# Attention with a top-2 mixture of experts on one core: two tiles' scores moved in TensorE's steady order, and one tile's masking moved on VectorE

## The chip, the cores and the metric

One core of one Trainium2 chip. The metric is the device time of one execution in microseconds. The engines are named as in the profile: PE (TensorE matmuls), PEld (TensorE weight loads), DVE (VectorE), ACT (ScalarE), POOL (GpSimd), SP (SyncE, which here only issues DMAs).

## What is computed

The input x is 8 batches x 512 rows x 128 columns, fp32. With B = 8, T = 512:

```python
xn = layernorm(x)
q, k, v = xn @ Wq.T, xn @ Wk.T, xn @ Wv.T
attn = (q @ k.T) * tril(ones)            # masked scores become 0, not -inf
attn = softmax(attn / sqrt(T)) @ v
gates = softmax(xn @ Wg)                 # 8 experts, the two largest kept, renormalized
ffn = sum_e gate[e] * (xn @ We[e] + be[e])
out = x + attn + ffn
```

A masked score is zero and still takes part in the softmax, so each row also gets exp(-max) times the sum of the values behind the diagonal. The kernel adds that, and the expert biases, with one small matmul per batch (the bias product).

## The kernel before, in words

All inputs lie in SBUF from the start (one DMA per batch of x). A batch has four tiles of 128 rows. The five engines each run a list written out by hand, and they meet only at semaphores. A batch n goes through these steps; each is a function in the engine's section.

- TensorE: `transpose_x` (L302), `project_u` (u = x Wq.T Wk, L310 to L313), `wide(n, k, t)` with k = C (values, last expert, gates; 264 columns), A (four experts, 512 columns) and B (three experts, 384 columns), `scores(n, t)` (128(t+1) columns), `transpose_probs` (L277), `attend` (L293; fp32, two matmul instructions for each of its t+1 products), `value_sums` (L320), `transpose_rows` (L328) and `bias` (L334). `wide` and `scores` go through the helper `three` (L239, L240, L243): operands split into a high and a low part, three matmuls. The wide blocks, X, U, SV and DT share a ring of four PSUM banks, the scores have three banks, and attention products and the bias product gather in one bank, `attb`.
- VectorE: `mask_scores` (L560: masks the scores in PSUM and takes their maximum; a second instruction reads the accumulator), `negate_max` (L567), the gate's steps (L491 to L528), `mix_b` (L543), `sv_rows` (L608), `finish_tile` (L597: `attb` times 1/sum plus the experts' part, into the output tile), `x_lo` and `u_lo` (L480), `normal_stats` (L465).
- ScalarE: `softmax_exp` (L840), `probs_copy` (L855), `scale_experts` (L829), `c_copy` (L813), `sv_high` (L880), `rows_copy` (L886), `normalize` (L801), `x_hi` (L867), `u_hi` (L859).
- GpSimd: `sum_experts` (L1010 to L1017), `bias_rows` (L1029 to L1041, five small operations that make the left operand of the bias product), `normal_rstd`, `scale_last`.

The waits around the change:

- `transpose_rows(b)` waits for a free bank of the ring and for `rows_ready`, which L1041 sets.
- `bias_rows(b)` follows `sum_experts(b, 2)` on GpSimd, whose last operation (L1017) waits for `mix_ready` of tile 2, and it waits for `tot_ready` too.
- `bias(b)` waits for `sv_rows_ready` and for `dt_ready` (ScalarE's copy of the transposed rows).
- `attend(b, t)` waits for `pt_ready` (ScalarE's copy of the transposed probabilities). `attend(b, 0)` starts a new accumulation in `attb` and waits for all four `finish_tile` of the batch before.
- `finish_tile(b, 0)` waits for the bias product.
- `scores(b, 0)` waits for both parts of u and, as all scores, for `pt_ready` of three tiles before (three banks).
- `transpose_x(b+1)` needs the bank that `sv_rows(b, ...)` reads.

The steady loop is `for n in range(1, B - 1)`, six rounds (n = 1 to 6), the same on every engine. Batch 0 and the last batch have orders of their own. A round mixes the end of batch n-1 with the beginning of batch n.

Of the kernel before, what the change touches and what calls it, by code (L numbers as in the profile page):

```python
# [81 lines left out]
def build(nc, x, w_attention, w_stacked, be, shapes, out):  # L82
# [10 lines left out]
    with ExitStack() as ctx:  # L93
# [129 lines left out]
        def _(pe):  # L223
# [21 lines left out]
            def wide(b, k, t):  # L245

                ring_free(f"{k}{t}", b)
                if t == 0 and k == "C":

                    pe.wait_ge(S["xh_ready"], b + 1)  # L250
                    if b == 0:
                        pe.wait_ge(S["wcl_ready"], 1)
                if t == 0 and k in "AB" and b == 0:

                    pe.wait_ge(S["wla_ready" if k == "A" else "wlb_ready"], 1)
                c = slice(OFF[k], OFF[k] + COLS[k])
                r = slice(t * P, (t + 1) * P)
                three(bank(f"{k}{t}", b)[:, 0:COLS[k]], xT_hi[:, b % 2, r], xT_lo[:, b % 2, r], w_hi[:, c], w_lo[:, c],
                      (S["xl_ready"], b + 1) if t == 0 and k == "C" else None).then_inc(S["wide_done"], 1)

            def scores(b, t):

                if t == 0:
                    pe.wait_ge(S["uh_ready"], b + 1)
                if b * NT + t >= SCORE_BANKS:

                    pe.wait_ge(S["pt_ready"], b * NT + t + 1 - SCORE_BANKS)
                r, n = slice(t * P, (t + 1) * P), (t + 1) * P
                three(score_bank(b, t)[:, 0:n], uT_hi[:, b % 2, r], uT_lo[:, b % 2, r], xT_hi[:, b % 2, 0:n],
                      xT_lo[:, b % 2, 0:n], (S["ul_ready"], b + 1) if t == 0 else None).then_inc(S["scores_done"], 1)  # L270
# [9 lines left out]
            def attend(b, t):  # L280

                pe.wait_ge(S["pt_ready"], b * NT + t + 1)
                if t == 0:
                    pe.wait_ge(S["c_used"], b * NT + NT)
                    if b == 0:

                        pe.wait_ge(S["be_ready"], 1)
                    if b > 0:

                        pe.wait_ge(S["fin_done"], b * NT)  # L290
                for j in range(t + 1):

                    last = nc.tensor.matmul(attb[:, t * P:(t + 1) * P], probT[:, b % 2, t, j * P:(j + 1) * P],  # L293
                                            c_s[:, b % 2, j, 0:P], start=(t == 0), stop=False, skip_group_check=True)
                last.then_inc(S["pv_done"], 1)
# [34 lines left out]
            def bias(b):  # L330

                pe.wait_ge(S["sv_rows_ready"], b + 1)
                pe.wait_ge(S["dt_ready"], b + 1)
                nc.tensor.matmul(attb[:], lhsT_rows[:], rhs_rows[:].rearrange("p t h -> p (t h)"),  # L334
                                 start=False, stop=True, skip_group_check=True).then_inc(S["bias_done"], 1)
# [54 lines left out]
            for n in range(1, B - 1):  # L390
                wide(n, "C", 3)
                wide(n - 1, "B", 2)
                wide(n - 1, "B", 3)
                attend(n - 1, 1)
                scores(n, 0)
                transpose_probs(n - 1, 2)
                wide(n - 1, "A", 3)
                transpose_probs(n - 1, 3)
                value_sums(n)
                attend(n - 1, 2)  # L400
                scores(n, 1)
                transpose_rows(n - 1)
                attend(n - 1, 3)
                bias(n - 1)
                wide(n, "A", 0)
                wide(n, "B", 0)
                scores(n, 2)
                transpose_x(n + 1)
                transpose_probs(n, 0)
                wide(n, "A", 1)  # L410
                wide(n, "B", 1)
                attend(n, 0)
                transpose_probs(n, 1)
                wide(n + 1, "C", 0)
                project_u(n + 1)
                scores(n, 3)
                wide(n + 1, "C", 1)
                wide(n + 1, "C", 2)
                wide(n, "A", 2)
# [38 lines left out]
        def _(dve):  # L458
# [72 lines left out]
            def mix_b(b, t, i):  # L531

                if i == 0:
                    dve.wait_ge(S["wide_done"], wide_count("B", b, t))
                    if t == 0:
                        dve.wait_ge(S["gate_ready"], b + 1)
                    if b > 0:

                        dve.wait_ge(S["ffn_ready"], (b - 1) * NT + t + 1)
                else:  # L540
                    chain.need(cnt["mix", b, t, i - 1])
                before = tile_ap(b, t) if i == 0 else mix[:, t, i - 1, :]
                ins = nc.vector.scalar_tensor_tensor(mix[:, t, i, :], bank(f"B{t}", b)[:, i * P:(i + 1) * P],  # L543
                                                     gate[:, b % 2, t, 4 + i:5 + i], before, ALU.mult, ALU.add)
                if i < 2:
                    cnt["mix", b, t, i] = chain.mark(ins)
                else:
                    ins.then_inc(S["mix_ready"], 1)

            def mask_scores(b, t):  # L550

                dve.wait_ge(S["scores_done"], b * NT + t + 1)
                if t == 0 and b > 1:

                    dve.wait_ge(S["exp_done"], (b - 1) * NT)
                    dve.wait_ge(S["em_done"], b - 1)
                n = (t + 1) * P
                cnt["maxed", b, t] = chain.mark(nc.vector.tensor_tensor_reduce(  # L560
                    score_bank(b, t)[:, 0:n], score_bank(b, t)[:, 0:n], causal[:, (NT - 1 - t) * P:], SCALE,
                    0.0 if t < NT - 1 else -3e38, ALU.mult, ALU.max, accum_out=mx[:, b % 2, t:t + 1]))

            def negate_max(b, t):

                chain.need(cnt["maxed", b, t])
                nc.vector.tensor_scalar(nmx[:, b % 2, t:t + 1], mx[:, b % 2, t:t + 1], -1.0, None, ALU.mult  # L567
                                        ).then_inc(S["nmx_ready"], 1)
# [31 lines left out]
            def sv_rows(b, t):  # L600

                if t == 0:
                    dve.wait_ge(S["svh_ready"], b + 1)
                    if b > 0:

                        dve.wait_ge(S["bias_done"], b)
                r = slice(t * ROWS, t * ROWS + G_ROW)
                ins = nc.vector.scalar_tensor_tensor(rhs_rows[r, t, :], sv_hi[r, :].bitcast(F32), shapes_s[r, P:P + 1],  # L608
                                                     bank("SV", b)[r, 0:P], ALU.mult, ALU.add)
                if t == NT - 2:  # L610
                    ins.then_inc(S["sv_rows_ready"], 1)
# [71 lines left out]

            for n in range(1, B - 1):
                mask_scores(n - 1, 2)
                mix_b(n - 1, 1, 0)
                normal_stats(n + 1, 0)
                mix_b(n - 1, 1, 1)
                negate_max(n - 1, 2)
                mix_b(n - 1, 1, 2)  # L690
                normal_stats(n + 1, 1)
                normal_stats(n + 1, 2)
                u_lo(n)
                mask_scores(n - 1, 3)
                mix_b(n - 1, 2, 0)
                negate_max(n - 1, 3)
                mix_b(n - 1, 2, 1)
                normal_stats(n + 1, 3)
                gate_max(n)
                mix_b(n - 1, 3, 0)  # L700
                gate_drop(n)
                gate_below(n)
                softmax_sum(n - 1)
                mix_b(n - 1, 2, 2)
                softmax_tot(n - 1)
                normal_finish(n + 1)
                mix_b(n - 1, 3, 1)
                gate_sum(n)
                mix_b(n - 1, 3, 2)
                mask_scores(n, 0)  # L710
                softmax_rec(n - 1)
                negate_max(n, 0)
                gate_rec(n)
                mask_scores(n, 1)
                negate_max(n, 1)
                finish_tile(n - 1, 0)
                gate_out(n)
                sv_rows(n, 0)
                sv_rows(n, 1)
                sv_rows(n, 2)  # L720
                mix_b(n, 0, 0)
                finish_tile(n - 1, 1)
                mix_b(n, 0, 1)
                finish_tile(n - 1, 2)
                mix_b(n, 0, 2)
                finish_tile(n - 1, 3)
                x_lo(n + 1)
# [405 lines left out]
```

## Time and profile before

| | before |
|---|---|
| runs of the kernel, us | 132.51, 132.60, 130.95 (median 132.51) |
| profiled execution, us | 132.71 |
| its span, us | 130.7 (so 2.0 us lie around it) |
| PE busy | 121.3 us, 93% |
| PEld busy | 109.1 us, 83% |
| DVE busy | 102.1 us, 78% |
| ACT busy | 101.4 us, 78% |
| POOL busy | 96.2 us, 74% |
| granted TensorE clock | 1.00 throughout |

The span runs from the first to the last instruction of the program. An engine's busy time is the union of its records. Matmul records overlap their successors, and their ends are modelled, so a gap shorter than a record does not show as idle. Times in the rows below are microseconds from the start of the span. A group such as "x6" is six instructions in a row merged, with the time from the first start to the last end.

### The profile page before, as it was taken

To read this page: it belongs to the slowest core of one execution; us is meant where nothing else is said; L and a number is where in the kernel's file an instruction comes from. 1 tells how busy PE (TensorE), PEld (TensorE's weight loads), DVE (VectorE), ACT (ScalarE), POOL (GpSimd) and SP (SyncE) were. 2 spreads that over 40 slices of the span, in tenths; PEclk is the share of its full clock that TensorE was granted. 3 is DMA by queue.
4 is the path that set the end of the run, shared out by engine and by line. 5 is a ranking of instruction groups with operands and counts; after the bars stand their busy time and mean duration, and the time that the engine had idled before them with its cause. 6 is when DMAs were issued, how large, how long until landed. Compare 5 with 4: busy or idle time off the path is not lost.

```text
span 130.7 us, 3014 instructions
## 1 busy us (share of the span) xinstructions
PE 121.3 (93%) x766; PEld 109.1 (83%) x766; DVE 102.1 (78%) x507; ACT 101.4 (78%) x341; POOL 96.2 (74%) x216
## 2 busy tenths in 40 slices
PE   4839999999999999999999999999999999999870
PEld 4717878998989989999899999999899899888650
DVE  0477789797988799697969796979877985967822
ACT  2145699979986999789996999699869999656850
POOL 7080228669995998689967997799859986788881
PEclk9999999999999999999999999999999999999999
DMA  2996000000020002000200020000200020002002
GB/s 65 362 295 164 0 0 8 0 3 3 10 70 5 3 0 80 0 0 3 82 3 3 0 78 10 0 0 7 78 5 0 0 80 0 0 5 83 3 0 80
DMA packets 8929, 5.18 MB, mean 40 GB/s; under 512 B 328, under 2 KB 8784, under 8 KB 8912
## 3 DMA queue, kind: packets, MB, share of 16 engines
q1 hardware_dynamic: 8608, 4.79, 12.5%
q10 hardware_dynamic: 304, 0.20, 0.5%
q8 instruction: 6, 0.10, 0.3%
q14 instruction: 11, 0.09, 0.2%
HBM read 2.89 MB, written 2.10 MB: 38 GB/s over the span
## 4 chain that ended last, share of the span: by engine, by line
PE 83%; DVE 7%; DMA 3%; POOL 2%; ACT 1%; issue 1%; POOLq 0%
PE ring L239 13%; PE ring L240 13%; PE ring L243 13%; PE attb L293 12%; PE score L277 6%; PE ring L320 4%; PE score L243 4%; PE score L240 4%; PE score L239 3%; DMA x_all<-in_x_dram 3%; PE ring L302 2%; PE ring L310 2%; PE ring L313 2%; PE ring L311 2%; DVE xn L648 2%; PE ring L328 1%
## 5 line engine op out<-in xcount | busy, mean ns | idle before, releaser
L829 ACT ACTIVATE ysc<-ring,gate 128x128 f32<-128x128 f32 x128 | 36.4, 372 | 3.4 <-DVE gate L528 1.5
L239 PE MATMUL ring<-w_hi,xT_hi 128*128 128x264 f32 (+2 forms) x96 | 35.2, 367 | 0.6 <-DVE mix L543 0.4
L240 PE MATMUL ring<-w_lo,xT_hi 128*128 128x264 f32 (+2 forms) x96 | 33.0, 344 | 0.0
L243 PE MATMUL ring<-w_hi,xT_lo 128*128 128x264 f32 (+2 forms) x96 | 32.9, 343 | 0.0
L1010 POOL TENSOR_TENSOR ysc<-ysc 128x256 f32<-128x256 f32 x32 | 23.5, 734 | 7.3 <-ACT ysc L829 7.3
L293 PE MATMUL attb<-c_s,probT 128*128 128x128 f32 x160 | 23.3, 278 | 0.0
L543 DVE SCALAR_TENSOR_TENSOR mix<-ring,gate,mix 128x128 f32<-128x128 f32 x64 | 22.0, 344 | 0.2
L239 PEld LDWEIGHTS ring<-w_hi,xT_hi 128*128 128x128 f32 x96 | 18.7, 194 | 3.3 <-DVE mix L543 0.6
L293 PEld LDWEIGHTS attb<-c_s,probT 128*128 128x128 f32 x160 | 20.8, 191 | 0.4
L240 PEld LDWEIGHTS ring<-w_lo,xT_hi 128*128 128x128 f32 x96 | 18.6, 194 | 1.6
L243 PEld LDWEIGHTS ring<-w_hi,xT_lo 128*128 128x128 f32 x96 | 18.5, 193 | 1.4
L1017 POOL TENSOR_TENSOR ffn<-ysc,mix 128x128 f32<-128x128 f32 x32 | 14.6, 457 | 6.5 <-DVE tot L582 4.3
L840 ACT ACTIVATE prob<-score,nmx 128x128 f32<-128x128 f32 (+3 forms) x32 | 17.4, 542 | 0.6 <-DVE nmx L567 0.6
L543 DVE SCALAR_TENSOR_TENSOR mix<-ring,gate,x_all 128x128 f32<-128x128 f32 x32 | 11.0, 345 | 7.9 <-PE ring L243 7.7
L597 DVE SCALAR_TENSOR_TENSOR o_s<-attb,rinv,ffn 128x128 f32<-128x128 f32 x32 | 10.8, 344 | 8.0 <-PE attb L334 7.9
L1013 POOL TENSOR_TENSOR ysc<-ysc,y 128x128 f32<-128x128 f32 x32 | 14.7, 461 | 2.5
L1011 POOL TENSOR_TENSOR ysc<-ysc 128x128 f32<-128x128 f32 x32 | 14.7, 459 | 2.5
L560 DVE CUSTOM_DVE_ANT_0 score<-score,causal 128x128 f32<-128x128 f32 (+3 forms) x32 | 15.7, 490 | 0.1
L990 POOL TENSOR_TENSOR rstd<-veps,half 128x4 f32<-128x4 f32 x8 | 8.1, 1014 | 9.5 <-DVE veps L475 5.9
L277 PE MATMUL score<-ident,prob 128*128 128x128 f32 x80 | 14.2, 276 | 0.2 <-ACT prob L840 0.2
L855 ACT COPY probT<-score 128x128 f32<-128x128 f32 (+3 forms) x32 | 13.8, 430 | 0.4 <-PE score L277 0.3
L801 ACT ACTIVATE xn<-x_all,nmr,rstd 128x128 f32<-128x128 f32 x29 | 12.0, 483 | 1.6 <-POOL nmr L998 1.6
(99 smaller groups left out, 248.9 us busy)
## 6 DMA issues: line engine op xcount, KB each, us to landing
x_all<-in_x_dram SPq DMA_DIRECT2D x8, 256.0 KB, 5.9
out_dram<-o_s SPq DMA_DIRECT2D x7, 256.0 KB, 2.3
w_f<-in_w_stacked_dram SPq DMA_DIRECT2D x1, 580.0 KB, 5.2
out_dram<-o_s SPq DMA_DIRECT2D x1, 192.0 KB, 2.1
wqk_s<-in_w_attention_dram ACTq DMA_DIRECT2D x1, 128.0 KB, 3.7
shapes_s<-in_shapes_dram ACTq DMA_DIRECT2D x1, 64.5 KB
out_dram<-o_s SPq DMA_DIRECT2D x1, 64.0 KB, 1.8
be_s<-in_be_dram ACTq DMA_DIRECT2D x1, 4.0 KB
```

The lines of the kernel that those rows point to most:

```text
L239: nc.tensor.matmul(dst, hi, w_h, start=True, stop=False)
L240: nc.tensor.matmul(dst, hi, w_l, start=False, stop=False)
L243: return nc.tensor.matmul(dst, lo, w_h, start=False, stop=True)
L277: last = nc.tensor.transpose(score_bank(b, t)[:, c], prob[:, t, c], ident[:])
L293: last = nc.tensor.matmul(attb[:, t * P:(t + 1) * P], probT[:, b % 2, t, j * P:(j + 1) * P], c_s[:, b % 2, j, 0:P], start=(t == 0), stop=F ...
L543: ins = nc.vector.scalar_tensor_tensor(mix[:, t, i, :], bank(f"B{t}", b)[:, i * P:(i + 1) * P], gate[:, b % 2, t, 4 + i:5 + i], before, AL ...
L560: cnt["maxed", b, t] = chain.mark(nc.vector.tensor_tensor_reduce(score_bank(b, t)[:, 0:n], score_bank(b, t)[:, 0:n], causal[:, (NT - 1 - t ...
L829: last = nc.scalar.mul(ysc[:, t, e, :], bank(f"A{t}", b)[:, e * P:(e + 1) * P], gate[:, b % 2, t, e:e + 1])
L840: nc.scalar.activation(prob[:, t, 0:n], score_bank(b, t)[:, 0:n], ACT.Exp, bias=nmx[:, b % 2, t:t + 1], scale=1.0, accum_out=rs[:, b % 2, ...
L1010: chain.step(nc.gpsimd.tensor_tensor(y[:, 0:2, :], y[:, 0:2, :], y[:, 2:4, :], ALU.add))
L1011: chain.step(nc.gpsimd.tensor_tensor(y[:, 0, :], y[:, 0, :], y[:, 1, :], ALU.add))
L1013: chain.step(nc.gpsimd.tensor_tensor(y[:, 0, :], y[:, 0, :], y7[:, b % 2, t, :], ALU.add))
```

## The change

Three edits. In TensorE's steady round, `scores(n, 0)` goes ahead of `attend(n-1, 1)`, and `scores(n, 1)` goes from between `attend(n-1, 2)` and `transpose_rows(n-1)` to behind `bias(n-1)`. In VectorE's steady round, `mask_scores(n, 1)` and `negate_max(n, 1)` go from ahead of `finish_tile(n-1, 0)` to behind `sv_rows(n, 2)`. `mask_scores` waits, from the third batch on, also for the negated maximum of the same tile two batches before.

```diff
@@ TensorE, steady round
                 wide(n - 1, "B", 3)
+                scores(n, 0)
                 attend(n - 1, 1)
-                scores(n, 0)
                 transpose_probs(n - 1, 2)
                 wide(n - 1, "A", 3)
                 transpose_probs(n - 1, 3)
                 value_sums(n)
                 attend(n - 1, 2)
-                scores(n, 1)
                 transpose_rows(n - 1)
                 attend(n - 1, 3)
                 bias(n - 1)
+                scores(n, 1)
                 wide(n, "A", 0)
@@ mask_scores
                 dve.wait_ge(S["scores_done"], b * NT + t + 1)
+                if b > 1:
+                    dve.wait_ge(S["nmx_ready"], (b - 2) * NT + t + 1)
@@ VectorE, steady round
                 negate_max(n, 0)
                 gate_rec(n)
-                mask_scores(n, 1)
-                negate_max(n, 1)
                 finish_tile(n - 1, 0)
                 gate_out(n)
                 sv_rows(n, 0)
                 sv_rows(n, 1)
                 sv_rows(n, 2)
+                mask_scores(n, 1)
+                negate_max(n, 1)
                 mix_b(n, 0, 0)
```

## Rows read from the trace of the kernel before

**Rows 1.** Busy time by stretch, one steady round (from-to length, engine busy)

```profile
45.15:59.06 13.91, 13.91 (x97) 12.79 (x95) 11.94 (x62) 12.19 (x42) 11.53 (x25) 1.00 0.06 19
```

**Rows 2.** Timeline of PE, 56.9 to 59.6: start, length, line, what

```profile
56.93 0.83 PE L293 MATMUL attb<-c_s,probT 128*128 128x128 f32 x6
57.52 0.36 PE L239 MATMUL score<-xT_hi,uT_hi 128*128 128x256 f32 x1
57.72 0.28 PE L240 MATMUL score<-xT_lo,uT_hi 128*128 128x256 f32 x1
57.83 0.28 PE L243 MATMUL score<-xT_hi,uT_lo 128*128 128x256 f32 x1
...
58.02 0.30 PE L328 MATMUL ring<-ident,lhs_rows 128*128 128x128 f32 x1
...
59.06 0.48 PE L334 MATMUL attb<-rhs_rows,lhsT_rows 128*128 128x512 f32 x1
```

**Rows 3.** Timeline of PEld, around L328 in a steady round and in the tail

```profile
57.72 0.19 PEld L243 LDWEIGHTS score<-xT_hi,uT_lo 128*128 128x128 f32 x1
...
57.99 0.14 PEld L328 LDWEIGHTS ring<-ident,lhs_rows 128*128 128x128 f32 x1
...
58.14 0.19 PEld L293 LDWEIGHTS attb<-c_s,probT 128*128 128x128 f32 x1
...
113.39 0.30 PEld L293 LDWEIGHTS attb<-c_s,probT 128*128 128x128 f32 x2
113.94 0.14 PEld L328 LDWEIGHTS ring<-ident,lhs_rows 128*128 128x128 f32 x1 [0.24 <-issue]
```

**Rows 4.** Timeline of POOL, the same two places

```profile
56.42 0.46 POOL L1017 TENSOR_TENSOR ffn<-ysc,mix 128x128 f32<-128x128 f32 x1 [0.52 <-DVE tot L582]
...
57.63 0.25 POOL L1041 TENSOR_TENSOR lhs_rows<-gate_tot,lhs_rows 128x32 fp32r<-128x32 f32 x1
...
113.56 0.26 POOL L1041 TENSOR_TENSOR lhs_rows<-gate_tot,lhs_rows 128x32 fp32r<-128x32 f32 x1
```

**Rows 5.** Timeline of ACT, 57.4 to 58.1

```profile
57.48 0.61 ACT L855 COPY probT<-score 128x512 f32<-128x512 f32 x1
```

**Rows 6.** Timeline of DVE, 53.7 to 58.8

```profile
53.71 0.35 DVE L543 SCALAR_TENSOR_TENSOR mix<-ring,gate,x_all 128x128 f32<-128x128 f32 x1 [1.05 <-PE ring L243]
...
55.94 0.34 DVE L543 SCALAR_TENSOR_TENSOR mix<-ring,gate,mix 128x128 f32<-128x128 f32 x1
...
58.15 0.43 DVE L560 CUSTOM_DVE_ANT_0 score<-score,causal 128x256 f32<-128x256 f32 x1
58.50 0.14 DVE L560 DVE_READ_ACCUMULATOR2_ANT mx<- 128x1 f32 x1
58.68 0.15 DVE L567 TENSOR_SCALAR nmx<-mx 128x1 f32<-128x1 f32 x1
```

**Rows 7.** Timeline of DVE, 59.5 to 63.3, behind the bias product

```profile
59.58 0.35 DVE L597 SCALAR_TENSOR_TENSOR o_s<-attb,rinv,ffn 128x128 f32<-128x128 f32 x1 [0.75 <-PE attb L334]
...
59.95 1.04 DVE L608 SCALAR_TENSOR_TENSOR rhs_rows<-sv_hi,shapes_s,ring 3x128 fp32r<-3x128 f32 x3
61.02 0.35 DVE L543 SCALAR_TENSOR_TENSOR mix<-ring,gate,x_all 128x128 f32<-128x128 f32 x1
...
62.32 0.34 DVE L597 SCALAR_TENSOR_TENSOR o_s<-attb,rinv,ffn 128x128 f32<-128x128 f32 x1
62.58 0.68 DVE L480 TENSOR_TENSOR xT_lo<-ring,xT_hi 128x512 fp32r<-128x512 f32 x1
```

**Rows 8.** Timeline of PE and PEld, 62.7 to 63.1, at `attend(n, 0)`

```profile
62.72 0.34 PE L243 MATMUL ring<-w_hi,xT_lo 128*128 128x384 f32 x1
62.90 0.38 PE L293 MATMUL attb<-c_s,probT 128*128 128x128 f32 x2
...
62.78 0.31 PEld L293 LDWEIGHTS attb<-c_s,probT 128*128 128x128 f32 x2
```

## The prediction

> **What bounds the kernel now.** I read the stretches first, one from bias product to bias product. A round of the steady loop takes 13.9 us, and in it TensorE (PE) is covered by matmul records from end to end, while VectorE (DVE) and GpSimd (POOL) are busy for 11.9 and 11.5 us and the granted clock is 1.00, the 2.4 GHz level [rows 1]. There are six such rounds, n = 1 to 6. So any time that TensorE gains or loses in a round is paid six times, unless it was already waiting there. The records overlap, however (six products of 128 columns take 0.83 us together, 0.11 us from start to start, though each is recorded for 0.27) [rows 2], so waits shorter than a record do not show as idle time. They show in the order of the weight loads and of the ends. That is the second view.
>
> Weight loads normally start with the matmul in front: that of L243 starts at 57.72, as does the matmul L240. The one of the rows' transpose, L328, starts at 57.99, 0.16 us after the matmul L243 at 57.83 [rows 2, 3]. What let it go is in the third view: L1041 on GpSimd, the last operation of `bias_rows`, ends at 57.63 + 0.25 = 57.88, 0.11 us earlier [rows 4]. In the tail the same pair stands at 113.82 and 113.94, and there no scores lie in front of L328: the weight load before it began about 113.5 and the trace itself shows 0.24 us of idle time [rows 3, 4]. The distance is 0.11 to 0.12 us in seven of the eight batches (the eighth, at the very end, is later). So in every round `transpose_rows` already waits for GpSimd, and the second tile's scores stand in front of it as cover. Behind it the first weight load of `attend(n-1, 3)` starts at 58.14, 0.05 us behind the end (57.48 + 0.61 = 58.09) of ScalarE's copy L855 of tile 3's probabilities: a second release, 0.15 us after the first [rows 3, 5].
>
> Where do these two releases hang? DVE waits 1.05 us for the matmuls of `wide(n-1, "B", 2)` (B2) and goes at 53.71. From there its list runs without a stop to the last `mix_b` of tile 2 at 55.94; 0.14 us after its end POOL starts L1017 (56.42), then the five operations of `bias_rows` [rows 4, 6]. The copy L855 hangs on the same list, through the gate exponential that ScalarE waits for. So L328 comes 4.3 us after the end of B2, whatever TensorE does between.
>
> **The change part by part.** First, `scores(n, 0)` ahead of `attend(n-1, 1)`. The same instructions between the same neighbours; what changes is how often TensorE passes between the fp32 and the split kind of matmul. At such a passage the first record begins early (57.52) and lasts 0.36 instead of 0.28 us, but the ends are regular: the sixth product ends at 57.76, the three scores at 57.88, 58.00 and 58.11 [rows 2]. That is 0.12 us each, no price for the passage. Ends of the range: a gain of 0.08 us for each of the four passages that the two moves save (if the longer record were a cost), 1.9 us in all, or a loss of the same size. I take 0, since the ends say so. `mask_scores(n, 0)` keeps its place on DVE and starts no earlier.
>
> Second, `scores(n, 1)` from ahead of `transpose_rows` to behind `bias`. It takes away 58.11 - 57.76 = 0.35 us in front of a transpose that is held until 57.99 anyway, so L328, the eight products of `attend(n-1, 3)` and the bias product stay where they are with respect to B2; the hole in front of L328 only grows from 0.1 to about 0.45 us. Behind the bias product the same three matmuls now stand in front of `wide(n, "A", 0)`, with nothing to cover. Matmuls run in order, so what is queued behind L328 (products, bias, scores) cannot fill the hole. Cost: +0.35 us a round. Bounds: 0.16 (if the transpose came earlier by all of its present wait, which would need GpSimd to be earlier) and 0.36.
>
> Third, `mask_scores(n, 1)` and `negate_max(n, 1)` on DVE. Now they lie at 58.15, in 0.75 us of idle time ahead of `finish_tile(n-1, 0)`, which waits for the bias product; they cost nothing there [rows 6, 7]. Afterwards they stand behind the three `sv_rows`, in a stretch without idle time that runs from 59.58 on [rows 7]. Their price there: 0.35 from the start of the mask to that of its accumulator read, 0.18 on to the negation, and 0.11 to the next operation (I take that from what the pairs of small operations show; it lies between 0.07 and the 0.15 that the negation lasts), 0.64 us in all. Bounds: 0.60, and 0.72 if none of the three overlapped (0.43 + 0.14 + 0.15) [rows 6]. Everything behind comes 0.64 us later after the bias product: `mix_b(n, 0, ...)`, three `finish_tile`, `x_lo(n+1)`. The last `finish_tile(n-1, 3)` matters: it ends at 62.32 + 0.34 = 62.66, and `attend(n, 0)`, which overwrites `attb`, has its weight load at 62.78, 0.12 us behind that end and 0.06 us behind the matmul L243 of 62.72 that it would otherwise start with [rows 7, 8]. So this wait is on the edge already, hidden by the 0.18 us that L243 streams. With the change TensorE comes there 0.35 us later and the last `finish_tile` 0.64 us later. The weight load goes at 62.78 + 0.64 = 63.42, a matmul can follow it after 0.10 us or so (62.78 to 62.90 now) at 63.52, and it was due at 62.90 + 0.35 = 63.25. That is +0.27 us a round; with 0.60 to 0.72 for the price on DVE it is 0.22 to 0.35, and 0 if something I can't see gives DVE its time back.
>
> The Trainium skill bears on that price: "VectorE: DVE Perf Modes", section "The DRAIN you can't avoid", says that the next operation does not start until the pipeline of the one before is empty. The trace differs: the accumulator read starts at 58.50 while the mask is recorded until 58.58 [rows 6]. By the page the operations would stand end to end, and the change would cost an estimated 0.5 us more over six rounds.
>
> What is late next: `x_lo(n+1)` ends at 62.58 + 0.68 = 63.26 [rows 7], afterwards 63.90; the first C matmuls that need it come 0.62 us later as well, so the distance stays nearly what it is. `mask_scores(n, 1)` finds its scores long done, and `softmax_exp(n, 1)` on ScalarE comes more than half a microsecond after the new `nmx`. Before the next B2, DVE waits 1.05 us [rows 6], so the 0.64 us go no further than that.
>
> Fourth, the added wait of `mask_scores` for `nmx_ready` of two batches before. It is met long since. `mix_b` at 61.02, with three such waits, starts 0.02 us later than the pitch of the operations ahead of it (0.35) would put it [rows 7]; so 0 to 0.02 us, and I take 0.
>
> No DMA is issued by a moved step. Stores go out with the last `finish_tile`, under a microsecond later, and nothing waits for them before the next batch but one.
>
> Sum: (0.35 + 0.27) x 6 rounds = 3.7 us. The last batch has its own order, which is not touched. The profiled execution took 132.71 us with a span of 130.7; that gives 136.4. It stands 0.20 us above the median of the runs, so I forecast **136.2 us**. With the bounds of the DVE price it is 135.9 to 136.7.
>
> **The rivals.**
> (A) Not slower: L328 was not held by GpSimd; the 0.16 us in front of it and the 0.09 us that the first product behind it ends late are the price of a transpose right behind the scores. Then the move takes that away: L328 goes at 57.49, and the bias product ends 0.54 us earlier. TensorE would gain 0.19 us a round, but the chain from the bias product over `finish_tile` gets 0.64 longer and eats it: -0.54 + 0.64 - 0.02 = +0.08 a round, 0.5 us in all, 133.0. It decides if L328 follows the products at 0.11 us. For it: the scores are indeed what stands in front. Against it: the constant 0.11 us to L1041, and the tail, where no scores stand there and the wait is longer. 0.09.
> (B) Only the cover is lost and the later `finish_tile` is hidden, because DVE catches up in the stretch from 59.58 on: 0.35 x 6 = 2.1 us, 134.6. For it: the 0.64 us are put together from rows of another place. Against it: no idle time in that stretch. 0.14.
> (C) More: the mask in the tight stretch costs nearer 0.9 than 0.64 us, or `x_lo` also holds the third C matmul. Each 0.1 us on DVE is 0.6 us in all once `attend(n, 0)` waits; with 0.25 more it is 1.5 us, 137.7. For it: the distance of `x_lo` is small. Against it: the mask's duration hardly varies. 0.09.
> (D) Faster: the saved passages are worth the 0.08 us that the longer record suggests and (A) holds too: 133.0 - 1.9 = 131.1, which is still less than 2% below. Beyond 2%: 0.03.
>
> **How the numbers follow.** My forecast has 0.65. Within 2% (a measurement of this kernel can hardly tell less from no change; 2% above is 135.2) lie (A) and (B), 0.23; slower by more are the forecast and (C), 0.74; faster 0.03. The range 134.0 to 137.4 takes in the forecast and (B), and leaves out (A), (D) and most of (C), 0.2 at most.
>
> **What would show it.** Right: rounds of 14.5 us between bias products; about 0.6 us between the weight loads of the last product of `attend(n-1, 2)` and L328, with L328 still 0.11 us behind L1041; a wait at the weight load of `attend(n, 0)` of 0.3 us beside its neighbours, 0.12 us behind L597; DVE's wait for the bias product grown to some 1.5 us. Wrong: L328 at 0.11 us behind the products, GpSimd's L1041 earlier with respect to B2, or rounds of 14.3 us with no wait at `attend(n, 0)`. It would also be wrong if DVE's wait at B2 vanished.

## The result, and the profile after

The changed kernel takes 136.81 us (median of 4 runs, 136.38 to 137.02) against 132.56 us (4 runs, 130.95 to 132.65): ratio 1.034, 95% interval 1.028 to 1.040. A second measurement (e8 below) gave 1.031, interval 1.026 to 1.036. The forecast was 136.2 us in a range of 134.0 to 137.4. The profiled execution took 136.69 us with a span of 134.7 us, 4.0 us more than before.

One round, from bias product to bias product, by stretch (length, then busy time of PE, PEld, DVE, ACT, POOL, the granted clock, DMA):

```profile
45.75:60.31 14.56, 14.23 (x97) 12.85 (x95) 11.92 (x62) 12.38 (x42) 11.49 (x25) 1.00 0.06 19
```

It answers to [rows 1]: 14.6 us instead of 13.9, with nearly the same work on every engine (the largest difference is 0.19 us on ACT) and the same granted clock. PE now has 0.33 us of idle time that its records show.

The same places on TensorE, timeline of PE, of the changed kernel (line numbers behind 554 are two higher than before):

```profile
58.20 0.83 PE L293 MATMUL attb<-c_s,probT 128*128 128x128 f32 x6
59.27 0.30 PE L328 MATMUL ring<-ident,lhs_rows 128*128 128x128 f32 x1 [0.24 <-POOL lhs_rows L1043]
...
64.33 0.34 PE L243 MATMUL ring<-w_hi,xT_lo 128*128 128x384 f32 x1
64.73 0.46 PE L293 MATMUL attb<-c_s,probT 128*128 128x128 f32 x2
```

and of PEld:

```profile
59.24 0.14 PEld L328 LDWEIGHTS ring<-ident,lhs_rows 128*128 128x128 f32 x1 [0.40 <-DVE mix L543]
...
64.70 0.30 PEld L293 LDWEIGHTS attb<-c_s,probT 128*128 128x128 f32 x2 [0.36 <-issue]
```

The transpose L328 now follows the products of `attend(n-1, 2)` directly and starts 0.24 us behind their last end (58.20 + 0.83), where [rows 2] had the scores. The view of PE names GpSimd's L1043, the former L1041, as what released it; it ends 0.11 us ahead of the weight load (58.87 + 0.26 = 59.13):

```profile
58.87 0.26 POOL L1043 TENSOR_TENSOR lhs_rows<-gate_tot,lhs_rows 128x32 fp32r<-128x32 f32 x1
```

The view of PEld puts the same wait down to VectorE's `mix_b` (L543). That was not it: in e5 below L328 starts before the last of these operations does (57.99 and 58.04) and 0.01 us before the one ahead of it ends, still 0.11 us behind L1043. At `attend(n, 0)` L293 starts 0.40 us behind L243; it was 0.18 [rows 8]. (Over the rounds it is 0.42 and 0.175, middle values.) Its two products also stand 0.18 apart instead of 0.11.

DVE behind the bias product (answers to [rows 7]; the wait at L599 was 0.75):

```profile
60.82 0.35 DVE L599 SCALAR_TENSOR_TENSOR o_s<-attb,rinv,ffn 128x128 f32<-128x128 f32 x1 [1.43 <-PE attb L334]
...
61.19 1.04 DVE L610 SCALAR_TENSOR_TENSOR rhs_rows<-sv_hi,shapes_s,ring 3x128 fp32r<-3x128 f32 x3
62.26 0.43 DVE L562 CUSTOM_DVE_ANT_0 score<-score,causal 128x256 f32<-128x256 f32 x1
62.72 0.08 DVE L562 DVE_READ_ACCUMULATOR2_ANT mx<- 128x1 f32 x1
62.84 0.15 DVE L569 TENSOR_SCALAR nmx<-mx 128x1 f32<-128x1 f32 x1
62.95 0.35 DVE L543 SCALAR_TENSOR_TENSOR mix<-ring,gate,x_all 128x128 f32<-128x128 f32 x1
...
64.25 0.34 DVE L599 SCALAR_TENSOR_TENSOR o_s<-attb,rinv,ffn 128x128 f32<-128x128 f32 x1
```

From the start of the three `sv_rows` to that of the first `mix_b` it is 62.95 - 61.19 = 1.76 us; before it was 61.02 - 59.95 = 1.07 [rows 7]. The moved masking costs 0.68 us there (0.69 by these rounded starts). The last `finish_tile` ends at 64.59, and the weight load at 64.70 follows it by 0.115 us, as before.

**Two stretches.** For all kernels below I measured the same two distances in every round of the profiled execution. Stretch 1 goes from the start of the `mix_b` for which DVE waited (the end of B2) to the weight load of L328, stretch 2 from the end of the bias product L334 to the end of the last `finish_tile` of that batch. For the kernel before: 57.99 - 53.71 = 4.28 and 62.66 - 59.54 = 3.12 [rows 3, 6, 7]. For the changed kernel: 59.24 - 54.96 = 4.28 and 64.59 - 60.79 = 3.80. Rounds are from bias start to bias start, so the first of them holds the end of round 1 of the loop and most of round 2; the figures are middle values of rounds 2 to 6 of the loop, in us, and agree from round to round within 0.08 unless said. Each ratio is taken against runs of the kernel before that were made beside that version (medians of 132.25 to 132.69 us for e1 to e12).

| kernel | stretch 1 | stretch 2 | round | ratio to before, 95% interval |
|---|---|---|---|---|
| before | 4.28 | 3.12 | 13.90 | 1 |
| changed | 4.28 | 3.80 | 14.59 | 1.034 (1.028 to 1.040) |
| e1 first scores alone | 4.30 | 3.12 | 13.91 | 1.002 (0.998 to 1.006) |
| e2 masking alone | 4.29 | 3.81 | 14.60 | 1.031 (1.025 to 1.037) |
| e3 second scores alone | 4.29 | 4.18 | 14.95 | 1.046 (1.040 to 1.052) |
| e4 changed, finish one slot earlier | 4.30 | 3.50 | 14.40 | 1.021 (1.015 to 1.026) |
| e5 changed, earlier release | 3.84 | 4.00 | 14.51 | 1.025 (1.021 to 1.029) |
| e6 before, earlier release | 4.15 | 3.27 | 13.86 | 0.995 (0.991 to 0.998) |
| e7 changed, no added wait | 4.29 | 3.80 | 14.59 | 1.032 (1.025 to 1.038) |
| e8 changed again | 4.29 | 3.80 | 14.59 | 1.031 (1.026 to 1.036) |
| e9 before, statistics later | 4.30 | 3.12 | 13.87 | 0.998 (0.995 to 1.002) |
| e10 = e9 + finish one slot earlier | 4.31 | 2.86 | 13.88 | 0.999 (0.995 to 1.003) |
| e11 = changed + edits of e10 | 4.28 | 3.49 | 14.28 | 1.016 (1.011 to 1.021) |
| e12 before, sums first | 4.15 | 3.28 | 13.89 | 1.001 (0.997 to 1.004) |

(In e9 and e10 one round of the profiled execution is 0.17 us longer than the others, with stretch 1 at 4.46; the middle values leave it out. The first round of e5 is 14.35 us, that of e12 13.74; both are taken up below.)

The rest of the round is TensorE's way from the weight load of L328 to the bias product and from the last `finish_tile` to B2. The first part is 1.07 us before, after and in e1 to e4, e7 and e8; it is 1.26 in e5, 1.03 in e6, 0.98 in e9 to e11 and 1.05 in e12, because ScalarE's copy L855 holds the first product behind L328 in all but e6 and e9 to e11. From the end of the bias product to B2 it is 8.08 us before and 8.76 in the changed kernel: the whole 0.68 us lie there.

### The profile page after: what moved, and what is told of

Its sections match the earlier page's. It is cut to its first block, busy times and chain, and to the rows that moved or that the text cites. A ratio compares the mean times of both kernels' runs of the same rounds, so it can differ in the third digit from the quotient of the medians.

```text
span 134.7 us, 3038 instructions
## 1 busy us (share of the span) xinstructions
PE 123.3 (92%) x766; PEld 109.6 (81%) x766; DVE 102.0 (76%) x507; ACT 102.5 (76%) x341; POOL 96.2 (71%) x216
## 4 chain that ended last, share of the span: by engine, by line
PE 64%; DVE 16%; POOL 7%; issue 5%; ACT 3%; DMA 3%; POOLq 1%
PE ring L239 11%; PE ring L243 11%; PE ring L240 11%; PE attb L293 8%; DVE mix L543 4%; DVE kept L498 3%; PE score L243 3%; PE score L240 3%; PE score L239 3%; DMA x_all<-in_x_dram 3%; PE score L277 2%; PE ring L302 2%; ACT ysc L831 2%; DVE stats L465 2%; DVE top L491 2%
## 5 line engine op out<-in xcount | busy, mean ns | idle before, releaser
L243 PE MATMUL ring<-w_hi,xT_lo 128*128 128x264 f32 (+2 forms) x96 | 33.2, 345 | 0.0
L293 PE MATMUL attb<-c_s,probT 128*128 128x128 f32 x160 | 24.0, 283 | 0.5
L293 PEld LDWEIGHTS attb<-c_s,probT 128*128 128x128 f32 x160 | 20.4, 191 | 2.4 <-issue 2.3
L543 DVE SCALAR_TENSOR_TENSOR mix<-ring,gate,mix 128x128 f32<-128x128 f32 x64 | 22.0, 344 | 0.2
L599 DVE SCALAR_TENSOR_TENSOR o_s<-attb,rinv,ffn 128x128 f32<-128x128 f32 x32 | 10.8, 345 | 11.9 <-PE attb L334 11.8
L243 PEld LDWEIGHTS ring<-w_hi,xT_lo 128*128 128x128 f32 x96 | 18.6, 194 | 1.4
L1019 POOL TENSOR_TENSOR ffn<-ysc,mix 128x128 f32<-128x128 f32 x32 | 14.6, 457 | 6.5 <-DVE tot L584 4.3
L543 DVE SCALAR_TENSOR_TENSOR mix<-ring,gate,x_all 128x128 f32<-128x128 f32 x32 | 11.1, 346 | 7.8 <-PE ring L243 7.7
L1013 POOL TENSOR_TENSOR ysc<-ysc 128x128 f32<-128x128 f32 x32 | 14.7, 459 | 2.5
L857 ACT COPY probT<-score 128x128 f32<-128x128 f32 (+3 forms) x32 | 13.7, 429 | 0.6 <-PE score L277 0.5
L815 ACT COPY c_s<-ring 128x264 f32<-128x264 f32 x32 | 11.8, 393 | 2.7 <-PE ring L243 2.7
```

Source lines behind the costliest of these rows:

```text
L243: return nc.tensor.matmul(dst, lo, w_h, start=False, stop=True)
L1013: chain.step(nc.gpsimd.tensor_tensor(y[:, 0, :], y[:, 0, :], y[:, 1, :], ALU.add))
```

## The experiments

**e1: is a passage between fp32 and split matmuls worth something?**

```diff
                 wide(n - 1, "B", 3)
+                scores(n, 0)
                 attend(n - 1, 1)
-                scores(n, 0)
```

> The kernel before with scores(n, 0) ahead of attend(n-1, 1), nothing else. Theory (a passage between fp32 and split matmuls costs nothing): rounds of 13.9 us, 132.5 us, ratio 1.000 within 0.3%. Rival (each saved passage is worth the 0.08 us by which the first record is longer, two a round): 0.16 us a round less, 131.6 us, ratio 0.993.

Measured: 132.64 us (12 runs) against 132.69 (17 runs), ratio 1.002, interval 0.998 to 1.006; rounds of 13.91 us. The 0.993 of the rival is outside the interval. So the first edit costs and brings nothing that these runs can tell. It has two of the four passages; the other two moved with the second edit.

**e2: the masking alone.**

```diff
                 gate_rec(n)
-                mask_scores(n, 1)
-                negate_max(n, 1)
                 finish_tile(n - 1, 0)
...
                 sv_rows(n, 2)
+                mask_scores(n, 1)
+                negate_max(n, 1)
```

> The kernel before with mask_scores(n, 1) and negate_max(n, 1) behind sv_rows(n, 2), TensorE's order untouched. Theory (the stretch from the bias product to attend(n, 0) is set by VectorE's list alone, and the two steps cost 0.68 us in it): the whole 0.68 us a round, 14.59 us from bias to bias, 136.6 us, ratio 1.031, as much as the full change. Rival (two costs that add, 0.35 us for the lost cover and 0.33 us for the later finish_tile): 0.33 us a round, 134.5 us, ratio 1.015.

Measured: 136.84 us, ratio 1.031 (1.025 to 1.037), rounds of 14.60 us. The whole loss of the change is there with TensorE's order untouched. Timeline of PE in e2, at `attend(n, 0)`:

```profile
63.20 0.34 PE L243 MATMUL ring<-w_hi,xT_lo 128*128 128x384 f32 x1
63.97 0.46 PE L293 MATMUL attb<-c_s,probT 128*128 128x128 f32 x2 [0.43 <-DVE o_s L597]
```

From start to start it is 0.77 us here and 0.42 in the changed kernel. The difference is the moved scores: they fill part of a hole that the masking has made. In the changed kernel the 0.35 us of the second scores are therefore not a cost of their own on top. Stretch 2 is as long with them as without (3.80 and 3.81), and the round with it.

**e3: the second scores alone,** with the masking left in front of `finish_tile(n-1, 0)`.

```diff
                 attend(n - 1, 2)
-                scores(n, 1)
                 transpose_rows(n - 1)
                 attend(n - 1, 3)
                 bias(n - 1)
+                scores(n, 1)
```

> The kernel before with scores(n, 1) behind bias(n-1) and the masking in its old place, so that VectorE's list waits there for scores that come behind the bias product. Theory (that stretch is VectorE's): finish_tile(n-1, 0) starts 0.35 us (the scores) + 0.68 us (masking) later after the bias product, rounds of 14.9 us, 138.7 us, ratio 1.047. Rival (only the cover is lost, VectorE has room): 0.35 us a round, 134.7 us, ratio 1.016.

Measured: 138.59 us, ratio 1.046 (1.040 to 1.052), rounds of 14.95 us. Timeline of DVE in e3:

```profile
60.66 0.43 DVE L560 CUSTOM_DVE_ANT_0 score<-score,causal 128x256 f32<-128x256 f32 x1 [1.79 <-PE score L243]
61.01 0.14 DVE L560 DVE_READ_ACCUMULATOR2_ANT mx<- 128x1 f32 x1
61.19 0.15 DVE L567 TENSOR_SCALAR nmx<-mx 128x1 f32<-128x1 f32 x1
61.37 0.35 DVE L597 SCALAR_TENSOR_TENSOR o_s<-attb,rinv,ffn 128x128 f32<-128x128 f32 x1
```

DVE waits for the scores behind the bias product and starts `finish_tile` only after the masking, 1.09 us behind the bias product's end (60.28) instead of 0.04. That is 1.05 us more, as forecast. Once the scores stand behind the bias product, the masking has to leave its old place. `attend(n, 0)` no longer shows that wait in its start (0.175 behind L243, as without a hold), because TensorE is held earlier, at `transpose_x(n+1)`, which needs the bank that `sv_rows` reads:

```profile
62.83 0.66 PE L302 MATMUL ring<-ident,xn 128*128 128x128 f32 x4 [0.47 <-DVE rhs_rows L608]
```

It starts 0.80 us behind the matmul in front instead of 0.17 (61.13 - 60.96 before). `sv_rows` comes later here by all that stands in front of `finish_tile`. In the changed kernel it does not, and there TensorE first meets VectorE at `attend(n, 0)`.

**e4: taking the last finish_tile off the path.** To the changed kernel:

```diff
-                mix_b(n, 0, 0)
                 finish_tile(n - 1, 1)
+                mix_b(n, 0, 0)
-                mix_b(n, 0, 1)
                 finish_tile(n - 1, 2)
+                mix_b(n, 0, 1)
-                mix_b(n, 0, 2)
                 finish_tile(n - 1, 3)
+                mix_b(n, 0, 2)
```

> The changed kernel with each of finish_tile(n-1, 1..3) in front of the mix_b step that stood before it, so that the last one ends 0.26 us earlier. Theory (attend(n, 0) waits for it): rounds 0.26 us shorter than the changed kernel's 14.59, 135.2 us, ratio to the kernel before 1.020. Rival (attend(n, 0) waits for something else, or x_lo(n+1) takes over at once): within 0.1 us a round of the changed kernel, 136.3 to 136.8 us, ratio 1.029 to 1.032.

Measured: 135.53 us, ratio 1.021 (1.015 to 1.026), rounds of 14.40 us. The last `finish_tile` ends 0.30 us earlier and the start of `attend(n, 0)` is free again (0.175 behind L243), so it was that wait. But of the 0.26 us expected, 0.19 come back. DVE and PEld of e4, two timelines:

```profile
64.10 0.68 DVE L480 TENSOR_TENSOR xT_lo<-ring,xT_hi 128x512 fp32r<-128x512 f32 x1
```

```profile
64.59 0.19 PEld L240 LDWEIGHTS ring<-w_lo,xT_hi 128*128 128x128 f32 x1
64.83 0.19 PEld L243 LDWEIGHTS ring<-w_hi,xT_lo 128*128 128x128 f32 x1
```

`x_lo(n+1)` ends at 64.78, and the weight load that reads it starts at 64.83 instead of 0.13 behind the one in front. This next wait, 0.1 us a round, is what the prediction's rival C named: the same 0.68 us of masking stand in front of it too.

**e7: the added wait.** The changed kernel without the two lines in `mask_scores`.

> The changed kernel without the added wait of mask_scores for nmx_ready. Theory (it is met long since): 136.6 us, within 0.2 us of the changed kernel, and the accumulator read still starts 0.45 us behind the mask. Rival (the wait is part of why the two steps cost 0.68 instead of 0.64 us): 0.04 us a round less, 136.4 us, with the read at 0.35 us behind the mask.

Measured: 136.68 us, ratio 1.032 (1.025 to 1.038), rounds of 14.59 us, stretch 2 still 3.80. The accumulator read stands 0.45 us behind the mask in e7 too (62.39 and 62.84), as in the changed kernel, so the wait is not why. It costs nothing.

**e8: the changed kernel again,** beside e5 to e7.

> The changed kernel itself, for comparison on the same chip. 136.7 us, ratio 1.032, rounds of 14.59 us.

Measured: 136.27 us, ratio 1.031 (1.026 to 1.036), rounds of 14.59 us.

**e5 and e6: is the hole in front of L328 a wait for GpSimd?** The same edit on the changed kernel (e5) and on the kernel before (e6). VectorE's list, then ScalarE's:

```diff
-                mix_b(n - 1, 3, 0)
-                gate_drop(n)
-                gate_below(n)
-                softmax_sum(n - 1)
                 mix_b(n - 1, 2, 2)
+                softmax_sum(n - 1)
+                mix_b(n - 1, 3, 0)
                 softmax_tot(n - 1)
+                gate_drop(n)
+                gate_below(n)
@@
-                gate_exp(n)
                 probs_copy(n - 1, 2)
                 scale_experts(n - 1, 3)
+                gate_exp(n)
                 probs_copy(n - 1, 3)
```

> The changed kernel with the two releases of L328 and attend(n-1, 3) made earlier with respect to B2: on VectorE mix_b(n-1, 2, 2), softmax_sum and softmax_tot ahead of gate_drop and gate_below; on ScalarE probs_copy(n-1, 2) and scale_experts(n-1, 3) ahead of gate_exp(n). Theory (the hole in front of L328 is the wait for GpSimd's L1043, which hangs on B2 through VectorE): L328 comes 0.2 to 0.3 us earlier after B2, rounds of about 14.33 us, 135.3 us, ratio to the kernel before 1.021. Rival (the hole belongs to TensorE itself): no change, 136.7 us, ratio 1.032.

> The kernel before with the same two reorderings and nothing of the change. Theory: the 0.19 us a round for which L328 and the first product of attend(n-1, 3) wait go away, rounds of 13.72 us, 131.4 us, ratio 0.991. Rival A of the prediction (they are the price of a transpose right behind the scores): no change, ratio 1.000. A second rival: the gate exponential, now later, delays VectorE's list up to finish_tile and the time is longer.

Measured: e5 135.48 us, ratio 1.025 (1.021 to 1.029), rounds of 14.51 us; e6 131.76 us, ratio 0.995 (0.991 to 0.998), rounds of 13.86 us. Timeline of POOL and of PEld in e5:

```profile
57.62 0.26 POOL L1043 TENSOR_TENSOR lhs_rows<-gate_tot,lhs_rows 128x32 fp32r<-128x32 f32 x1
```

```profile
57.26 0.75 PEld L293 LDWEIGHTS attb<-c_s,probT 128*128 128x128 f32 x6
57.99 0.14 PEld L328 LDWEIGHTS ring<-ident,lhs_rows 128*128 128x128 f32 x1
58.31 0.30 PEld L293 LDWEIGHTS attb<-c_s,probT 128*128 128x128 f32 x2 [0.18 <-ACT probT L857]
```

and PEld in e6, where the scores stand in front:

```profile
56.48 0.19 PEld L243 LDWEIGHTS score<-xT_hi,uT_lo 128*128 128x128 f32 x1
56.62 0.14 PEld L328 LDWEIGHTS ring<-ident,lhs_rows 128*128 128x128 f32 x1
56.72 0.41 PEld L293 LDWEIGHTS attb<-c_s,probT 128*128 128x128 f32 x3
```

In e5 L328 is still 0.11 us behind GpSimd's last operation (57.88), but both come 0.44 us earlier after B2 (3.84 instead of 4.28). In e6 GpSimd is done 0.4 us ahead, and L328 follows the scores by 0.14 us instead of 0.27, with the next load 0.10 behind. A transpose right behind the scores has no price above 0.03 us; rival A of the prediction falls. What is left in e5 in front of `attend(n-1, 3)` is the copy L857: its first weight load starts 0.05 us behind it and 0.34 behind L328 instead of 0.15, which takes back 0.19 of the 0.44 us.

Both came out short by half or more, though. The second stretch grew, by 0.20 us in e5 and by 0.15 in e6. DVE and POOL of e6 behind the bias product:

```profile
58.15 0.35 DVE L597 SCALAR_TENSOR_TENSOR o_s<-attb,rinv,ffn 128x128 f32<-128x128 f32 x1 [0.31 <-PE attb L334]
58.42 0.33 DVE L528 TENSOR_TENSOR gate<-gexp,grec 128x32 f32<-128x32 f32 x1
58.67 0.33 DVE L608 SCALAR_TENSOR_TENSOR rhs_rows<-sv_hi,shapes_s,ring 3x128 fp32r<-3x128 f32 x1
```

```profile
57.43 0.73 POOL L1010 TENSOR_TENSOR ysc<-ysc 128x256 f32<-128x256 f32 x1
58.24 0.47 POOL L1011 TENSOR_TENSOR ysc<-ysc 128x128 f32<-128x128 f32 x1
```

`gate_out` (L528) lasts 0.33 us instead of 0.18 and ends 0.04 us behind the end of GpSimd's L1011 (58.71). In the kernel before it starts between two operations of GpSimd and is not touched. GpSimd's list has moved further ahead than the bias product, and the two now meet. It is so in every full round of e6 (L528 ends 0.043 to 0.047 us behind L1011, five of five) and of e5 (behind L1013, 0.044 to 0.045, five of five). The second rival of e6, a later gate exponential, is not seen from the second round on: DVE still waits 0.31 us for the bias product. Two more VectorE operations are longer in e5 and e6 for the same reason as L528, `softmax_sum` (L577, 0.28 to 0.31 us instead of 0.15) and `softmax_tot` (L582, 0.35 or 0.36 instead of 0.15 in eleven rounds of twelve).

The first rounds, in which L528 kept its 0.18 us, do not agree. That of e5 is 14.35 us with stretch 2 at 3.80, as forecast. That of e6 is 13.91 us and not 13.72: there VectorE is still at its list when the bias product ends, without any wait, and the way from `attend(n, 0)` to B2 is 0.09 us longer than in its other rounds. Why was not found.

**e9 and e10: leaving the gate alone.** To the kernel before, e9:

```diff
-                normal_stats(n + 1, 3)
                 gate_max(n)
...
                 softmax_tot(n - 1)
+                normal_stats(n + 1, 3)
                 normal_finish(n + 1)
@@
-                gate_exp(n)
                 probs_copy(n - 1, 2)
+                gate_exp(n)
                 scale_experts(n - 1, 3)
```

> The kernel before with the chain from B2 to the two releases shortened without touching the gate: normal_stats(n+1, 3) moved behind softmax_tot(n-1) on VectorE, probs_copy(n-1, 2) ahead of gate_exp(n) on ScalarE. Theory (two stretches make the round: B2 to L328, held by GpSimd and ScalarE, and bias to attend(n, 0), held by VectorE): L328 and attend(n-1, 3) are held no more, the second stretch keeps its 3.12 us from the end of the bias product to the end of the last finish_tile, rounds of 13.72 us, 131.4 us, ratio 0.992. Rival (in e6 only half of it came because something else in the loop binds at 13.86): 13.86 us again, ratio 0.995.

> e9 and each of finish_tile(n-1, 1..3) one slot earlier, as in e4. Theory: TensorE already decides in both stretches, so no more than 0.03 us a round beside e9, ratio 0.991. Rival (the hold of attend(n, 0) costs more than it shows): another 0.1 us a round, ratio 0.987.

Measured: 132.10 us, ratio 0.998 (0.995 to 1.002), and 132.04 us, ratio 0.999 (0.995 to 1.003); rounds of 13.87 and 13.88 us. Stretch 2 stayed at 3.12, and e10 brought nothing over e9, as the theory had it. But stretch 1 did not shorten (4.30). The reason is on DVE, e9:

```profile
55.74 0.39 DVE L507 TENSOR_TENSOR below<-kept,top 128x32 f32<-128x32 f32 x1
56.06 0.15 DVE L577 TENSOR_TENSOR tot<-em,masked_keys 128x4 f32<-128x4 f32 x1
```

```profile
55.62 0.46 POOL L1013 TENSOR_TENSOR ysc<-ysc,y 128x128 f32<-128x128 f32 x1
```

The forecast rounds of 13.72 us did not come. `gate_below` came 0.2 us earlier after B2, into L1013 when 0.34 us of it were left (before it was 0.14), and lasted 0.39 us instead of 0.19, to 0.05 us behind L1013's end. What was moved out of the way came back as a longer operation, and all that is behind it on VectorE with it. `attend(n-1, 3)` did follow L328 at once (0.03 us instead of 0.15), which is worth 0.09 us; the round shows 0.03 of it, and most of the rest stands between the bias product and B2, 0.04 us more than before, for a reason not found.

**e11: both stretches on the changed kernel.** The changed kernel with the edits of e9 and e10.

> The changed kernel with the edits of e10. Theory (the two stretches account for the change): the first one shortens by 0.2 us (GpSimd's L1043), the second stays as in e4, where x_lo(n+1) holds TensorE after attend(n, 0); rounds of 14.40 - 0.22 = 14.18 us, 134.2 us, ratio 1.012. Rival (moving the scores costs TensorE something of its own): rounds of 14.4 us as in e4.

Measured: 134.21 us, ratio 1.016 (1.011 to 1.021), rounds of 14.28 us. Stretch 2 as in e4. Stretch 1 is not shorter, for the reason just shown; 0.09 of the 0.12 us beside e4 come from `attend(n-1, 3)`, whose probabilities are copied earlier now and which follows L328 at once. The part of the expectation on L1043 missed, so this run does not tell its rival by the round's length alone.

**e12: the sums first.** To the kernel before:

```diff
-                normal_stats(n + 1, 3)
                 gate_max(n)
+                mix_b(n - 1, 2, 2)
                 mix_b(n - 1, 3, 0)
-                gate_drop(n)
-                gate_below(n)
                 softmax_sum(n - 1)
-                mix_b(n - 1, 2, 2)
+                gate_drop(n)
                 softmax_tot(n - 1)
+                gate_below(n)
+                normal_stats(n + 1, 3)
                 normal_finish(n + 1)
@@
-                gate_exp(n)
                 probs_copy(n - 1, 2)
+                gate_exp(n)
```

> The kernel before; on VectorE mix_b(n-1, 2, 2) directly behind gate_max(n), softmax_sum(n-1) ahead of gate_drop(n), softmax_tot(n-1) between gate_drop and gate_below, normal_stats(n+1, 3) behind gate_below; on ScalarE probs_copy(n-1, 2) ahead of gate_exp(n). Theory (e9 missed because gate_below, whose two inputs lie in SBUF, was held until GpSimd's L1013 had ended, and all that is behind it on VectorE with it): GpSimd's rows come at least 0.3 us earlier after B2, gate_below starts behind L1013 and lasts 0.19 us, L328 follows the scores at 0.12 us, rounds of 13.74 us, 131.5 us, ratio 0.992. Rival (the chain is held elsewhere too): 13.86 us as in e9, ratio 0.998.

Measured: 132.43 us, ratio 1.001 (0.997 to 1.004), rounds of 13.89 us but for the first, which is 13.74. The first part of the theory held: rows 0.36 us ahead, `gate_below` 0.19 us long, L328 0.13 us behind the scores, stretch 1 at 4.15. The time did not follow. Stretch 2 is 3.28, because `gate_out` meets L1011 again:

```profile
60.22 0.34 DVE L528 TENSOR_TENSOR gate<-gexp,grec 128x32 f32<-128x32 f32 x1
```

```profile
60.04 0.47 POOL L1011 TENSOR_TENSOR ysc<-ysc 128x128 f32<-128x128 f32 x1
```

L528 ends 0.044 or 0.045 us behind L1011 in five rounds of five. The round of 13.74 us is the one in which L528 lasted 0.18 us (its start, 32.59, fell just before L1011 ended at 32.61) and stretch 2 was 3.13. So the forecast of 13.74 was met in the one round without the collision, and missed in the others.

e6 is the only version that is faster than the kernel before beyond its interval, by 0.5%, and faster than the changed kernel by 3 to 4%. A version that also keeps L528 clear of GpSimd was not run; by e12's first round it would gain about 0.15 us a round (an estimate; e6's first round, which had no collision either, did not gain it).

## Why the prediction was right

- **Rounds and places.** It put the loss into six equal rounds, 0.62 us each. It is 0.68 us, 4.1 us in all, against 4.0 us in the span; the rest is the part ahead of the first bias product (31.15 us instead of 31.24).
- **First edit at 0.** Right, by e1 for two of its four passages.
- **Second edit: L328 held by GpSimd, its distance to B2 fixed.** Right. Stretch 1 is 4.28 us with and without the scores in front, and the distance to L1041 / L1043 is 0.11 us in every round. e5 moved GpSimd's release and L328 moved with it.
- **Third edit: 0.64 us on VectorE.** The mechanism was right and this term was undersized: it is 0.68. The forecast took the distance from mask to accumulator read from [rows 6], 0.35; in the new place it is 0.46, and the negation follows 0.12 behind the read instead of 0.18. The added wait is not why (e7). What goes with it is the operation in front of the mask. Behind a `sv_rows` the read starts 0.02 us after the end of the mask in every steady round of the changed kernel, e2, e4 and e7, and behind any other operation 0.08 us before its end, in all masks of the kernel before. The last `sv_rows` writes from partition 64 on, most others from partition 0. No run tried which of these it is.
- **The hold at `attend(n, 0)`, +0.27 us.** It measured 0.33: 0.25 at the first product and 0.08 at the second, which the forecast had left out. The upper bound given was 0.35.
- **The sum 0.35 + 0.27.** Its total was close, but its two terms are not two causes. As written the hold was already net of the 0.35 us by which TensorE comes later. e2 shows what that means: masking alone costs the whole 0.68 us. Behind the bias product the second scores only fill time in which TensorE would wait for VectorE, and ahead of L328 they only filled time in which it waited for GpSimd. Had the masking been free, the scores should have cost their 0.35 by this account; no run has that case.
- **`x_lo` as what is late next.** Right in e4, where it took over at once.
- **The rivals.** (A) falls by e5 and e6, (B) by e2, where the later `finish_tile` alone costs 0.68 us, (D) with (A) and by e1. (C) asked for 0.9 us on VectorE; it was 0.68.
- **The Trainium skill's rule on back-to-back VectorE operations** ("VectorE: DVE Perf Modes", "The DRAIN you can't avoid"). The prediction took it to mean that all operations stand end to end. The same section says that a next operation that is not held starts earlier, and the trace of the changed kernel has both cases: each `finish_tile` still starts 0.26 us behind a `mix_b` that lasts 0.34, while the accumulator read now starts 0.02 us behind the end of the mask. So the 0.5 us that the prediction worked out from it were not what the page asks for.
- **Signs named.** The rounds (14.5 forecast, 14.59 measured), the 0.6 us between weight loads in front of L328 (0.59), the wait of 1.5 us on DVE (1.43) and a wait at B2 (1.02 against 1.05) were all found.

## What to carry to other kernels

An engine that is busy by the profile from end to end can still be led by others at two or three points of its loop. Measure, round by round, the distance from each release to the instruction it releases: where it is the same to 0.01 us, that is the path, and work moved from in front of one such point to behind another costs nothing or everything depending on what the other engine does there. Before moving a step into another engine's stretch, price it there, since a mask that filled idle time in one place cost 0.68 us a round in another. Small gains that shift two engines against each other should be read again for collisions, here VectorE operations with two inputs in SBUF against GpSimd's.

## What the runs showed of the hardware

- **A VectorE operation with two SBUF inputs waits for a GpSimd operation that is under way.** `gate_out` (L528) lasts 0.18 us alone. In e5, e6 and e12 it starts inside GpSimd's L1011 or L1013 with 0.26 us or more of it left, lasts 0.30 to 0.40 us and ends 0.043 to 0.047 us behind their end, in fifteen rounds of fifteen. In the tail of the kernel before it lasts 0.46 us, to 0.05 behind L1017. `gate_below` (L507) lasts 0.19 alone and 0.37 to 0.40 in the five rounds of each of e9, e10 and e11, ending 0.046 to 0.052 behind GpSimd's. `softmax_sum` and `softmax_tot` (128x4) last 0.15 alone and up to 0.43 when held, ending 0.016 to 0.023 behind. Over all traces these four operations start inside a GpSimd operation with 0.20 us or more left 104 times and are held each time; with 0.16 us or less left they keep their length, but for 0.02 us. So does one that is already running when GpSimd starts, as L528 in the kernel before. The Trainium skill has this sharing in "Advanced Engine Details and Errata", section "GPSIMD Details": the two engines share a read and a write interface, with conflicts for VectorE instructions with two SBUF inputs. The traces agree; that section gives the wait no length, the traces do. In e6 and in e12 stretch 2 is 0.15 us longer with it. This was read from the ends of the operations and from the one round of e12 without it; no run moved L528 alone.
- **The granted clock in the head.** In the profiled execution of the changed kernel and of e1 it is 0.67 from 6.5 to 13 us and 0.82 from there to 20 us, in e8 0.71 and 0.78: averages between the two levels of 1.2 and 2.4 GHz. In that of the kernel before it is 1.00. PE was busy for 4.2, 4.3 and 4.5 us of the 6.5 us ahead of the fall, and for 4.4 in the kernel before, which had none, so its busy time there does not tell them apart. e1 has it with the span of the kernel before (130.5 and 130.7 us), so it explains nothing of the difference; the first bias product ends no later for it.
- **Weight loads behind a release.** They start 0.05 us behind ScalarE's copy L855 and 0.11 to 0.12 us behind GpSimd's last operation and VectorE's last `finish_tile`, to within 0.003 us wherever they were held. It is not the releasing engine alone: behind VectorE's `x_lo` in e4 and its `sv_rows` in e3 it is 0.05 us too. Whether it is the number of waits in front of the instruction was not tried.
